# Narrow-matrix products on column tiles, with copy and transpose, and a TensorE sum for the last expert tile

## The chip, the cores and the metric

The kernel runs on one core of a Trainium2 chip. The metric is the device time of one launch in microseconds (us), lower is better. A core has five engines with queues of their own: TensorE (PE in the profile, its weight loads PEld), VectorE (DVE), ScalarE (ACT), GpSimd (POOL) and SyncE (SP), which here only issues loads and stores.

## The reference

Four batches of 512 rows of 128 values. First a cross attention with two heads of 64: keys and values are 77 context rows and the 512 rows of the batch itself. Then a mixture of eight experts of which each row takes two. Cut to its core:

```python
ln = layernorm(layernorm(x))              # latents, 512 x 128 a batch
xn = layernorm(ctx)                       # 77 x 96 a batch
q  = ln @ Wq.T
kv = concat([xn @ Wkv.T, ln @ Wlkv.T])
qn, kn = rmsnorm(q) * SCALE, rmsnorm(k)   # per head; rmsnorm needs the sum of squares of 64 values
attn = softmax(where(mask, qn @ kn.T, -big))
x = x + (attn @ v) @ Wo.T + bo
h = layernorm(x)
gates = softmax(h @ Wg + bg)              # 128 x 8
g, idx = top_k(gates, 2)
x = x + sum over the two of g * (h @ W[idx] + b[idx])
```

## The kernel before, in words

Each engine walks a list of jobs that is written out by hand in a string (TENSOR, VECTOR, SCALAR, GPSIMD). A job is a name, a part number p and a number n; a TENSOR job also names the banks of PSUM it writes (eight banks, "-" is the bank it already has). `free` (in the tensor block) makes a job wait until the former users of its banks are released, by the table RELEASED. All other order comes from semaphores that count jobs. So the lists set what is queued behind what.

The front (FRONT) has five parts: batch 0 in two halves of two tiles (p = 0, 1), then batches 1, 2 and 3 with four tiles of 128 rows each (p = 2, 3, 4). A part is normalized (`stats1` on VectorE, `rstd1` on GpSimd, `apply1` on ScalarE), transposed (`xT`, copied by `lnT`), and multiplied into `q`, `k` and `v`. Queries are squared (`qsq`), summed (`ssq`), their root taken on GpSimd (`rq`), scaled (`qn`), transposed (`qT`) and split in a high and a low half (`QH`, `QL`). Keys stay transposed: ScalarE squares them (`ksq`, inside job `k`), TensorE sums the squares of each head (`ssk`), VectorE makes means of the sums (`msk`) and GpSimd takes the root (`rk`), which is the scale of the exponentials.

In `ssk` the 128x128 tile of squared keys is the stationary matrix and `heads`, 128x2, is the moving one: four matmuls for a whole part, each of two passes in the trace, and the sums come out with rows on the partitions, as `msk` wants them (line 996). `gate` (line 1131) is built alike: four matmuls with the tile of normalized rows stationary and the 128x8 matrix `Wg0` moving; its logits go to VectorE (`logits`, `top`), with the exponential by ScalarE (`gexp`) in between, and give the weights `w`.

The rear (REAR) has one part for each batch. `score p n` (n = 0 to 4, the fifth are the context keys) takes three products for both heads; `exp` on ScalarE follows; `value p n` adds up; GpSimd and VectorE add the exponentials (`e01`, `e23`, `esum`), `den` sums them over the keys with 32 columns of ones stationary, each quarter on a column tile of its own (lines 1086 and 1091), ScalarE copies (`dens`) and `denT` transposes. `proj`, `x2`, `stats2`, `rstd2`, `apply2`, `l2T` (copied twice by ScalarE) and `l2L` lead to the experts.

The experts are computed for all rows: `low` and `high` are three matmuls of 512 columns each for four experts of one tile of rows. ScalarE scales the low four of each tile with four instructions (`low`, line 659), GpSimd adds these for a pair of tiles at once (`pair`: lines 470 and 471), VectorE scales and adds the high four with four dependent instructions for each tile (`high`, line 896), starting from `x2`, and GpSimd adds both (`res`, line 479). SyncE stores a pair of tiles after each `res`. GpSimd can't start `pair` until both tiles are scaled.

At the start, `warm` jobs are transposes of the identity that nobody reads. `ident` on GpSimd makes the identity matrix, `blanks` seven small constants; `ident` comes first. TensorE's first job waits for `ident`.

## Time and profile before

| what | value |
|---|---|
| median of 3 runs | 110.42 us (109.74 to 110.78) |
| the profiled execution | 110.81 us, its span 108.0 us |
| mean granted clock of TensorE | 0.991 |
| TensorE busy | 99.5 us (92%) |
| ScalarE busy | 83.2 us (77%) |
| GpSimd busy | 82.2 us (76%) |
| VectorE busy | 70.0 us (65%) |

The span is the time from the first to the last instruction; what lies around it is 2.8 us in this execution. The ends of matmuls are modelled, so the busy time of TensorE alone does not prove that it is the limit: its starts, and the lack of waits, have to be read with it. A time from the start of one job to the start of the next is called a step below.

### The profile page before, as it was taken

The page shows a single profiled execution, that of the slowest core. Times are in us where ns is not written, and L with a number is a line of the kernel's source. Part 1 is how long each engine was busy: PE and PEld are TensorE (multiplying, and loading weights), DVE is VectorE, ACT ScalarE, POOL GpSimd, SP SyncE. Part 2 cuts the span into 40 slices and gives each one's busy share as a digit, 9 for nine tenths or more (in the row PEclk, how much of TensorE's full clock was granted, in tenths as well). Part 3 has the DMA queues.
Part 4 walks back from the last instruction along what each step waited for, and adds up shares of the span by engine and source line. Part 5 has one row for each costly group of instructions (what it writes and reads, how often), then busy time and mean ns, then how long its engine had stood idle before and what let it go on. Part 6 is the DMA issues. An engine that isn't in the chain of part 4 may idle for free. (4 is left out here: it accounts for less than half of the span.)

```text
span 108.0 us, 2344 instructions
## 1 busy us (share of the span) xinstructions
PE 99.5 (92%) x674; PEld 69.4 (64%) x674; DVE 70.0 (65%) x327; ACT 83.2 (77%) x194; POOL 82.2 (76%) x85
## 2 busy tenths in 40 slices
...
DMA packets 6678, 3.90 MB, mean 36 GB/s; under 512 B 2314, under 2 KB 6282, under 8 KB 6667
## 3 DMA queue, kind: packets, MB, share of 16 engines
...
q10 hardware_dynamic: 832, 0.36, 1.2%
q8 instruction: 5, 0.08, 0.4%
...
HBM read 2.72 MB, written 1.05 MB: 35 GB/s over the span
## 5 line engine op out<-in xcount | busy, mean ns | idle before, releaser
L601 ACT ACTIVATE probs<-PS,shift,rk 128x512 f32<-128x512 f32 x32 | 22.5, 780 | 1.8 <-PE PS L1051 1.6
L659 ACT ACTIVATE scaled<-PS,w 128x128 f32<-128x128 f32 x64 | 17.5, 389 | 3.3 <-PE PS L920 1.9
L1072 PE MATMUL PS<-probs,V_sb 128*64 128x512 f32 x64 | 15.4, 602 | 0.0
L470 POOL TENSOR_TENSOR pair<-scaled 128x512 f32<-128x512 f32 x8 | 10.3, 1292 | 5.0 <-ACT scaled L659 4.4
L918 PE MATMUL PS<-WeH,l2H 128*128 128x512 f32 x32 | 13.3, 415 | 0.4 <-issue 0.4
L920 PE MATMUL PS<-WeH,l2L 128*128 128x512 f32 x32 | 12.6, 392 | 0.0
L919 PE MATMUL PS<-WeL,l2H 128*128 128x512 f32 x32 | 12.5, 390 | 0.0
L427 POOL TENSOR_TENSOR e<-probs,probs 128x1024 f32<-128x1024 f32 x4 | 9.5, 2368 | 3.8 <-ACT probs L601 3.8
L418 POOL TENSOR_TENSOR esum<-probs,probs 128x1024 f32<-128x1024 f32 x4 | 9.5, 2375 | 0.2 <-ACT probs L601 0.2
L457 POOL TENSOR_TENSOR l2L<-l2T,l2H 128x512 fp32r<-128x512 f32 x4 | 5.1, 1284 | 5.0 <-ACT l2H L642 5.0
L896 DVE SCALAR_TENSOR_TENSOR part<-PS,w,part 128x128 f32<-128x128 f32 x32 | 8.9, 342 | 0.0
L1072 PEld LDWEIGHTS PS<-probs,V_sb 128*64 128x64 f32 x64 | 4.1, 136 | 7.6 <-issue 7.4
L393 POOL TENSOR_TENSOR rq<-msq,half 128x8 f32<-128x8 f32 (+1 forms) x5 | 7.4, 1482 | 1.0 <-DVE msq L743 0.9
L399 POOL TENSOR_TENSOR rk<-msk,half 128x8 f32<-128x8 f32 (+1 forms) x5 | 6.9, 1389 | 1.5 <-DVE msk L759 1.5
L814 DVE TENSOR_TENSOR esum<-esum,e 128x1024 f32<-128x1024 f32 x4 | 5.0, 1249 | 4.0 <-POOL e L427 4.0
L628 ACT ACTIVATE l<-x,nm,rstd 128x127 f32<-128x127 f32 x16 | 6.6, 501 | 1.1 <-POOL nm L448 1.1
L927 PE MATMUL PS<-ident 128*128 128x128 f32 x27 | 6.0, 376 | 1.5 <-POOL ident L363 1.5
L918 PEld LDWEIGHTS PS<-WeH,l2H 128*128 128x128 f32 x32 | 6.0, 188 | 1.8 <-issue 0.6
L1051 PE MATMUL PS<-QH,KH 64*128 64x512 f32 x32 | 7.1, 443 | 0.0
L741 DVE TENSOR_REDUCE ssq<-qsq 128x8 f32<-128x512 f32 (+1 forms) x5 | 2.9, 578 | 6.2 <-ACT qsq L533 6.2
L920 PEld LDWEIGHTS PS<-WeH,l2L 128*128 128x128 f32 x32 | 6.0, 188 | 1.4
L919 PEld LDWEIGHTS PS<-WeL,l2H 128*128 128x128 f32 x32 | 6.0, 189 | 1.0
...
## 6 DMA issues: line engine op xcount, KB each, us to landing
...
```

Source lines behind the costliest of these rows:

```text
L393: pool.tensor_tensor(rq[:, b, a:e], msq[:, b, a:e], half[:, 0:H * (e - a)].rearrange("p (t h) -> p t h", h=H), ALU.pow).then_inc(rq_made, 1)
L418: pool.tensor_tensor(esum[p % 2][:, :, s], probs[p % 2][0][:, :, s], probs[p % 2][1][:, :, s], ALU.add).then_inc(e01_made, 1)
L427: pool.tensor_tensor(e23[:, :, s], probs[p % 2][2][:, :, s], probs[p % 2][3][:, :, s], ALU.add).then_inc(e23_made, 1)
L470: step(pool.tensor_tensor(pair[:], scaled[m % 2][:, :, 0:EH // 2], scaled[m % 2][:, :, EH // 2:EH], ALU.add))
L601: act.activation(probs[p % 2][n][:, h, s], ps[:, s], ACT.Exp, bias=shift[:, 0:1], scale=rk[:, b, n, h:h + 1]).then_inc(probs_made, 1)
L659: last = act.activation(scaled[m // 2 % 2][:, m % 2, e], ps[:, e], ACT.Copy, scale=w[:, m, e:e + 1])
L896: last = dve.scalar_tensor_tensor(dst, bank("high", p, 2 * n + k)[:, e * C:(e + 1) * C], w[:, m, EH + e:EH + e + 1], src, ALU.mult, ALU.add)
L918: pe.matmul(dst, lH, rH, start=True, stop=False)
L919: pe.matmul(dst, lH, rL, start=False, stop=False)
L920: return pe.matmul(dst, lL, rH, start=False, stop=True)
L1051: last = pe.matmul(bank("score", p, n, h)[0:P if n < T else M, 0:(e - a) * P], k, queries[r, b % 2, a * P:e * P], start=(step == 0), stop= ...
L1072: last = pe.matmul(bank("value", p, 0)[h * D:(h + 1) * D, s], v, pr, start=(n == 0), stop=(n == KT - 1))
```

## The change

`heads` and `Wg0` get 32 columns (the added ones are zeros). For the whole parts (p = 2, 3, 4) `ssk` takes `heads` as the stationary matrix and the 128 columns of squared keys as the moving one, four matmuls, each on its own column tile of 32, all into one bank. The result has rows of the batch along the columns, so ScalarE copies it to SBUF (`ssks`), TensorE transposes it (`sskT`), and `msk` reads the transposed one. `gate` of batches 0, 1 and 2 does the same with `Wg0` (`gates`, `gateT`). The two halves of batch 0 (`ssk`) and batch 3 (`gate`) stay as they were.

For the last tile of the last batch the high four experts are scaled by ScalarE (`high1`), and TensorE adds all eight scaled products with the identity as the stationary matrix (`sum 3 0` the low four, `sum 3 1` the high four); VectorE adds that to `x2` (`final`). The tile before it goes alone through VectorE (`high1`) and GpSimd (`pair1`, `res1`). The last pair of tiles is stored by two stores.

All four lists are written anew. Among the differences: `blanks` before `ident` on GpSimd; `warm 5` with six transposes and not four; all `score` jobs come before `low 0 1`; and batches 2 and 3 of the front are taken together.

```diff
 TENSOR = """
+    warm 4 1 7   q 0 0 4   k 0 0 5   v 0 0 6   q 1 0 7   ssk 0 0 0   k 1 0 2   v 1 0 3   warm 5 6 5   qT 0 0 5
+    xT 2 0 6   ssk 1 0 4   ctxT 0 0 0   qT 1 0 7   v 2 0 6   q 2 0 2   k 2 0 4   ctx_v 0 0 3   ctx_k 0 0 5
+    score 0 0 06   score 0 1 17   ssk 2 0 3   ctx_ss 0 0 4   maskT 0 0 5   score 0 2 06   score 0 3 34
+    sskT 2 0 5   qT 2 0 1   score 0 4 72   value 0 0 5   value 0 1 -   score 1 0 06   score 1 1 13   score 1 2 42
+    value 0 2 -   value 0 3 -   value 0 4 -   score 1 3 70   score 1 4 61   proj 0 0 32   value 1 0 4
+    value 1 1 -   den 0 0 5   value 1 2 -   denT 0 0 0   xT 3 0 7   value 1 3 -   xT 4 0 1   k 3 0 6   q 3 0 5
+    q 4 0 7   k 4 0 0   v 3 0 2   v 4 0 3   den 1 0 1   ssk 3 0 2   ssk 4 0 6   value 1 4 -   qT 3 0 0
+    sskT 3 0 2   l2T 0 0 5   denT 1 0 1   qT 4 0 3   sskT 4 0 7   score 2 0 26   score 2 1 07   gate 0 0 5
+    low 0 0 3   gateT 0 0 2   value 2 0 6   score 2 2 54   score 2 3 07   value 2 1 -   value 2 2 -
+    score 2 4 24   proj 1 0 50   score 3 0 73   value 2 3 -   value 2 4 -   score 3 1 24   score 3 2 37
+    score 3 3 01   den 2 0 5   score 3 4 62   proj 2 0 43   denT 2 0 7   low 0 1 5   low 0 2 0   low 0 3 1
+    high 0 0 2   high 0 1 6   high 0 2 3   l2T 1 0 4   high 0 3 7   value 3 0 5   value 3 1 -   value 3 2 -
+    value 3 3 -   gate 1 0 0   den 3 0 4   gateT 1 0 2   value 3 4 -   denT 3 0 6   l2T 2 0 1   proj 3 0 03
+    gate 2 0 7   high 1 0 4   gateT 2 0 5   low 1 0 2   low 1 1 1   low 1 2 7   high 1 1 0   high 1 2 3
+    high 1 3 6   high 2 0 2   low 1 3 1   low 2 0 7   l2T 3 0 0   low 2 1 4   low 2 2 1   gate 3 0 5   low 2 3 0
+    high 2 1 7   high 2 2 3   high 2 3 6   low 3 0 4   low 3 1 1   low 3 2 0   low 3 3 2   high 3 0 7
+    high 3 1 5   high 3 2 4   high 3 3 3   sum 3 0 6   sum 3 1 -
 VECTOR = """
+    consts 0 0   stats1 0 0   stats1 1 0   ln_gain 0 0   ctx_stats 0 0   stats1 2 0   ssq 0 0   gain 0 0   kL 0 0
+    ssq 1 0   shift 0 0   qn 0 0   msk 0 0   ctx_apply 0 0   qn 1 0   kL 1 0   msk 1 0   QL 0 0   stats1 3 0
+    QL 1 0   stats1 4 0   ssq 2 0   kL 2 0   ctx_kL 0 0   mask 0 0   ctx_ms 0 0   cbias 0 0   qn 2 0   msk 2 0
+    QL 2 0   esum 0 0   split 0 0   x2 0 0   stats2 0 0   esum 1 0   ssq 3 0   ssq 4 0   kL 3 0   kL 4 0   qn 3 0
+    qn 4 0   msk 3 0   QL 3 0   msk 4 0   QL 4 0   logits 0 0   top 0 0   x2 1 0   esum 2 0   stats2 1 0   x2 2 0
+    stats2 2 0   esum 3 0   high 0 0   high 0 1   logits 1 0   top 1 0   x2 3 0   stats2 3 0   logits 2 0
+    high 1 0   top 2 0   high 1 1   logits 3 0   high 2 0   top 3 0   high 2 1   high 3 0   high1 3 2   final 3 0
 SCALAR = """
+    weights 0 0   apply1 0 0   apply1 1 0   lnT 0 0   lnT 1 0   qsq 0 0   k 0 0   qsq 1 0   v 0 0   apply1 2 0
+    k 1 0   QH 0 0   lnT 2 0   v 1 0   QH 1 0   ctxT 0 0   v 2 0   weights2 0 0   qsq 2 0   k 2 0   ctx_v 0 0
+    ctx_k 0 0   exp 0 0   ssks 2 0   exp 0 1   exp 0 2   QH 2 0   exp 0 3   exp 0 4   exp 1 0   exp 1 1   exp 1 2
+    oT 0 0   exp 1 3   exp 1 4   apply1 3 0   dens 0 0   apply1 4 0   lnT 3 0   lnT 4 0   k 3 0   qsq 3 0
+    qsq 4 0   k 4 0   v 3 0   apply2 0 0   ssks 3 0   dens 1 0   v 4 0   QH 3 0   ssks 4 0   l2T 0 0   QH 4 0
+    exp 2 0   gates 0 0   oT 1 0   exp 2 1   gexp 0 0   exp 2 2   exp 2 3   low 0 0   exp 2 4   exp 3 0   oT 2 0
+    exp 3 1   exp 3 2   dens 2 0   exp 3 3   exp 3 4   apply2 1 0   low 0 1   low 0 2   l2T 1 0   low 0 3
+    apply2 2 0   gates 1 0   dens 3 0   oT 3 0   gexp 1 0   l2T 2 0   gates 2 0   low 1 0   low 1 1   low 1 2
+    apply2 3 0   gexp 2 0   low 1 3   l2T 3 0   low 2 0   low 2 1   low 2 2   low 2 3   gexp 3 0   low 3 0
+    low 3 1   low 3 2   low 3 3   high1 3 3
 GPSIMD = """
+    blanks 0 0   ident 0 0   rstd1 0 0   rstd1 1 0   ctx_rstd 0 0   rstd1 2 0   rq 0 0   rq 1 0   xbo 0 0
+    xbo 1 0   rk 0 0   rstd1 3 0   rk 1 0   rstd1 4 0   rq 2 0   ctx_rk 0 0   rk 2 0   e01 0 0   e23 0 0
+    shifted 0 0   e23 1 0   e01 1 0   xbo 2 0   rstd2 0 0   rq 3 0   rq 4 0   rk 3 0   l2L 0 0   rk 4 0   e01 2 0
+    e23 2 0   xbo 3 0   e01 3 0   rstd2 1 0   e23 3 0   rstd2 2 0   pair 0 0   res 0 0   pair 0 1   res 0 1
+    l2L 1 0   l2L 2 0   rstd2 3 0   pair 1 0   res 1 0   pair 1 1   l2L 3 0   res 1 1   pair 2 0   pair 2 1
+    res 2 0   res 2 1   pair 3 0   pair1 3 2   res 3 0   res1 3 2
...
-        Wg0 = sb("Wg0", [P, E])
+        Wg0 = sb("Wg0", [P, 32])
...
-        heads = sb("heads", [P, H])
+        heads = sb("heads", [P, 32])
...
+        ss_sb = sb("ss_sb", [P, P])
+        gate_sb = sb("gate_sb", [P, P])
...
+            if p < len(REAR) - 1:
+                held = bank("gateT", p, 0)
+                if n == 0:
+                    return held[:, 0:T * 32].rearrange("p (t k) -> p t k", k=32)[:, :, 0:E]
+                return held[:, T * 32 * n:T * 32 * n + T * E].rearrange("p (t e) -> p t e", e=E)
...
-            "ssk": lambda p, n: (msk_made, p + 1),
+            "ssk": lambda p, n: (ss_made, whole_before(p) + 1) if whole(p) else (msk_made, p + 1),
+            "sskT": lambda p, n: (msk_made, p + 1),
...
-            "gate": lambda p, n: (w_made, p + 1),
+            "gate": lambda p, n: (gates_made, p + 1) if p < len(REAR) - 1 else (w_made, p + 1),
+            "gateT": lambda p, n: (w_made, p + 1),
...
+                    last = b * T + i + 2 == B * T
                     sp.wait_ge(res_made, (b * T + i) // 2 + 1)
-                    sp.dma_start(ov[:, i:i + 2], x2[:, b, i:i + 2]).then_inc(stored, 16)
+                    tiles = slice(i, i + 1 if last else i + 2)
+                    sp.dma_start(ov[:, tiles], x2[:, b, tiles]).then_inc(stored, 16)
                     stores += 1
+            sp.wait_ge(final_made, 1)
+            sp.dma_start(ov[:, T - 1], x2[:, B - 1, T - 1]).then_inc(stored, 16)
+            stores += 1
             sp.wait_ge(stored, 16 * stores)
 
...
+                pool.memset(Wg0[:, E:32], 0.0)
...
+            def pair1_(p, n):
+
+                m = tile_number(p, n)
+                pool.wait_ge(scaled_made, m + 1)
+                pool.wait_ge(low_made, m // 2)
+                pool.wait_ge(res_made, m // 2 - 1)
+                part = scaled[m // 2 % 2][:, m % 2]
+                step(pool.tensor_tensor(pair[:, m % 2], part[:, 0:EH // 2], part[:, EH // 2:EH], ALU.add))
+                pool.tensor_tensor(low[m // 2 % 2][:, m % 2], pair[:, m % 2, 0], pair[:, m % 2, 1], ALU.add).then_inc(low_made, 1)
+
+            def res1_(p, n):
+
+                m = tile_number(p, n)
+                pool.wait_ge(low_made, m // 2 + 1)
+                pool.wait_ge(acc_made, m + 1)
+                pool.tensor_tensor(x2[:, m // T, m % T], low[m // 2 % 2][:, m % 2], acc[m // 2 % 2][:, m % 2],
+                                   ALU.add).then_inc(res_made, 1)
+
...
+            def ssks_(p, n):
+
+                act.wait_ge(ssk_done, p + 1)
+                if whole_before(p):
+                    act.wait_ge(sskT_done, whole_before(p))
+                act.copy(ss_sb[:], bank("ssk", p, 0)[:, 0:P]).then_inc(ss_made, 1)
...
+            def gates_(p, n):
+
+                act.wait_ge(gate_done, p + 1)
+                if p:
+                    act.wait_ge(gateT_done, p)
+                act.copy(gate_sb[:], bank("gate", p, 0)[:, 0:P]).then_inc(gates_made, 1)
...
+            def high1_(p, n):
+
+                m = tile_number(p, n)
+                act.wait_ge(high_done, m + 1)
+                act.wait_ge(w_made, p + 1)
+                ps = bank("high", p, n)[:].rearrange("p (e c) -> p e c", e=EH)
+                for e in range(EH):
+                    last = act.activation(scaled_high[:, e], ps[:, e], ACT.Copy, scale=w[:, m, EH + e:EH + e + 1])
+                last.then_inc(high_scaled, 1)
...
+            def high1_(p, n):
+
+                m = tile_number(p, n)
+                dve.wait_ge(w_made, p + 1)
+                dve.wait_ge(high_done, m + 1)
+                src = x2[:, m // T, m % T]
+                for e in range(EH):
+                    dst = part[m % 2][e][:] if e < EH - 1 else acc[m // 2 % 2][:, m % 2]
+                    if e == EH - 1:
+                        dve.wait_ge(res_made, m // 2 - 1)
+                    last = dve.scalar_tensor_tensor(dst, bank("high", p, n)[:, e * C:(e + 1) * C], w[:, m, EH + e:EH + e + 1], src,
+                                                    ALU.mult, ALU.add)
+                    if e < EH - 1:
+                        dve.wait_ge(dve_step, step(last))
+                    src = dst
+                last.then_inc(acc_made, 1)
+
+            def final_(p, n):
+
+                dve.wait_ge(x2_made, p + 1)
+                dve.wait_ge(sum_done, 1)
+                dve.tensor_tensor(x2[:, B - 1, T - 1], bank("sum", p, 0)[:, 0:C], x2[:, B - 1, T - 1], ALU.add).then_inc(final_made, 1)
...
+                if whole(p):
+                    for t in range(T):
+                        last = pe.matmul(bank("ssk", p, 0)[t * 32:(t + 1) * 32, 0:P], heads[:], ksq[:, b % 2, t * P:(t + 1) * P],
+                                         start=True, stop=True)
+                    last.then_inc(ssk_done, 1)
+                    return
                 for t in range(a, e):
                     last = pe.matmul(bank("ssk", p, 0)[:, (t - a) * H:(t - a + 1) * H], ksq[:, b % 2, t * P:(t + 1) * P],
-                                     heads[:], start=True, stop=True)
+                                     heads[:, 0:H], start=True, stop=True)
                 last.then_inc(ssk_done, 1)
+
+            def sskT_(p, n):
+                free("sskT", p, 0)
+                pe.wait_ge(ss_made, whole_before(p) + 1)
+                pe.transpose(bank("sskT", p, 0)[:, 0:P], ss_sb[:], ident[:]).then_inc(sskT_done, 1)
...
+                if p < len(REAR) - 1:
+                    for t in range(T):
+                        last = pe.matmul(bank("gate", p, 0)[t * 32:(t + 1) * 32, 0:P], Wg0[:], l2T[:, b % 2, t * P:(t + 1) * P],
+                                         start=True, stop=True)
+                    last.then_inc(gate_done, 1)
+                    return
                 for t in range(a, e):
                     last = pe.matmul(bank("gate", p, 0)[:, (t - a) * E:(t - a + 1) * E], l2T[:, b % 2, t * P:(t + 1) * P],
-                                     Wg0[:], start=True, stop=True)
+                                     Wg0[:, 0:E], start=True, stop=True)
                 last.then_inc(gate_done, 1)
+
+            def gateT_(p, n):
+                free("gateT", p, 0)
+                pe.wait_ge(gates_made, p + 1)
+                pe.transpose(bank("gateT", p, 0)[:, 0:P], gate_sb[:], ident[:]).then_inc(gateT_done, 1)
 
...
+            def sum_(p, n):
+
+                if n == 0:
+                    free("sum", p, 0)
+                    pe.wait_ge(scaled_made, B * T)
+                else:
+                    pe.wait_ge(high_scaled, 1)
+                parts = scaled[(B * T - 1) // 2 % 2][:, 1] if n == 0 else scaled_high
+                for e in range(EH):
+                    last = pe.matmul(bank("sum", p, 0)[:, 0:C], ident[:], parts[:, e], start=(n == 0 and e == 0),
+                                     stop=(n == 1 and e == EH - 1))
+                if n == 1:
+                    last.then_inc(sum_done, 1)
+
```

## Rows read from the trace of the kernel before

**Rows 1.** The page's first part: busy us, share of the span, instructions.
```profile
PE 99.5 (92%) x674; PEld 69.4 (64%) x674; DVE 70.0 (65%) x327; ACT 83.2 (77%) x194; POOL 82.2 (76%) x85
```

**Rows 2.** Busy time by stage, two stretches of five us (x is instructions).
```profile
70.00:75.00 5.00, 5.00 (x41) 2.85 (x41) 4.86 (x24) 1.74 (x5) 2.50 (x3) 1.00 0.00 0
...
95.00:100.00 5.00, 5.00 (x23) 4.13 (x22) 4.51 (x20) 3.29 (x14) 4.54 (x6) 1.00 0.08 26
```

**Rows 3.** Waits: who waited for what; total us, times, longest.
```profile
PEld PS L1072 <- issue: 9.7, 33, 0.4
...
PEld PS L1051 <- ACT probs L601: 1.6, 2, 0.8
```

**Rows 4.** Timeline of TensorE: start us, us, engine, line, operation, count.
```profile
36.15 0.64 PE L1086 MATMUL PS<-esum,ones 128*32 128x256 f32 x8
36.61 0.62 PE L1091 MATMUL PS<-probs,ones 77*32 77x256 f32 x8
37.15 1.05 PE L996 MATMUL PS<-heads,ksq 128*128 128x2 f32 x8
38.07 0.42 PE L1100 MATMUL PS<-ident,den_sb 128*128 128x128 f32 x2
38.32 0.60 PE L1005 MATMUL PS<-ident,qn 128*128 128x128 f32 x4
```

**Rows 5.** Timeline of TensorE around the third gate.
```profile
85.02 0.95 PE L1131 MATMUL PS<-Wg,l2T 128*128 128x8 f32 x8
85.83 0.49 PE L918 MATMUL PS<-WeH,l2H 128*128 128x512 f32 x1
```

**Rows 6.** Groups by line: busy us, mean ns; a 128x128 copy by ScalarE.
```profile
L500 ACT COPY WoT<-PS 128x128 f32<-128x128 f32 x1 | 0.3, 262 | 0.0
```

**Rows 7.** Timeline of the start, GpSimd, TensorE and ScalarE.
```profile
1.42 0.10 POOL L369 MEMSET cmv<- 77x4 f32 x1
...
1.90 0.21 POOL L372 MEMSET two<- 128x128 f32 x1
...
1.53 3.25 PE L927 MATMUL PS<-ident 128*128 128x128 f32 x14 [1.53 <-POOL ident L363]
...
4.57 0.42 PE L934 MATMUL PS<-ident,Wq_sb 128*128 128x128 f32 x1
...
5.45 0.48 ACT L495 COPY WT<-PS 128x384 f32<-128x384 f32 x1 [1.47 <-PE PS L936]
5.83 1.65 ACT L510 ACTIVATE xh<-x_sb,nm,rstd 128x128 f32<-128x128 f32 x4
```

**Rows 8.** Timeline of TensorE, the third part's queries and keys.
```profile
15.47 1.13 PE L968 MATMUL PS<-WT,lnT 128*128 128x128 f32 x8 [0.26 <-issue]
16.44 1.02 PE L977 MATMUL PS<-lnT,WT 128*128 128x512 f32 x2
```

**Rows 9.** Timeline of the tail, TensorE, ScalarE, VectorE and GpSimd.
```profile
100.68 0.39 PE L920 MATMUL PS<-WeH,l2L 128*128 128x512 f32 x1
...
101.36 0.39 PE L920 MATMUL PS<-WeH,l2L 128*128 128x512 f32 x1
...
99.07 2.17 ACT L659 ACTIVATE scaled<-PS,w 128x128 f32<-128x128 f32 x8 [0.43 <-PE PS L920]
...
103.85 0.60 DVE L896 SCALAR_TENSOR_TENSOR acc<-PS,w,part 128x128 f32<-128x128 f32 x2
...
104.44 1.40 POOL L479 TENSOR_TENSOR x<-low,acc 128x256 f32<-128x256 f32 x2
```

**Rows 10.** Timeline of the last batch's chain, VectorE, GpSimd, ScalarE.
```profile
79.07 1.13 DVE L829 SCALAR_TENSOR_TENSOR x2a<-PS,rden,xbo 128x128 f32<-128x128 f32 x4 [0.65 <-PE PS L1112]
...
82.79 0.15 DVE L848 TENSOR_REDUCE var<-mv 128x4 f32<-128x8 f32 x1
...
84.27 1.02 POOL L447 TENSOR_TENSOR rstd<-var,half 128x4 f32<-128x4 f32 x1
...
86.20 1.70 ACT L628 ACTIVATE l<-x,nm,rstd 128x127 f32<-128x127 f32 x4
```

More of the change, by code:

```diff
@@ L33 @@
-    score 1 1 14   score 1 2 07   value 0 2 -   value 0 3 -   value 0 4 -   score 1 3 14   score 1 4 07
-    den 0 0 5   ssk 3 0 6   denT 0 0 1   qT 3 0 4   proj 0 0 53   value 1 0 6   value 1 1 -   value 1 2 -
-    xT 4 0 0   score 2 0 74   score 2 1 21   score 2 2 35   k 4 0 0   q 4 0 4   den 1 0 7   score 2 3 12
-    score 2 4 07   value 1 3 -   value 1 4 -   value 2 0 3   denT 1 0 5   qT 4 0 1   ssk 4 0 2   proj 1 0 40
-    v 4 0 7   l2T 0 0 6   den 2 0 2   score 3 0 17   score 3 1 62   score 3 2 04   denT 2 0 5   low 0 0 1
@@ L38 @@
-    gate 0 0 7   score 3 3 26   value 2 1 -   value 2 2 -   value 2 3 -   value 2 4 -   value 3 0 0
-    score 3 4 42   proj 2 0 67   l2T 1 0 1   high 0 0 3   high 0 1 2   gate 1 0 4   den 3 0 1   value 3 1 -
-    value 3 2 -   value 3 3 -   value 3 4 -   denT 3 0 5   low 0 1 6   proj 3 0 71   low 0 2 2   low 0 3 3
-    low 1 0 0   l2T 2 0 4   high 0 2 6   high 0 3 2   low 1 1 1   low 1 2 5   low 1 3 7   gate 2 0 3   high 1 0 0
-    high 1 1 4   high 1 2 1   high 1 3 2   l2T 3 0 6   low 2 0 5   low 2 1 7   gate 3 0 0   low 2 2 4   low 2 3 6
@@ L660, in low_ @@
                 last.then_inc(scaled_made, 1)
-            walk(SCALAR, dict(apply2=apply2_, apply1=apply1_, weights=weights_, weights2=weights2_, lnT=lnT_, qsq=qsq_, QH=QH_, k=k_, v=v_, ctxT=ctxT_, ctx_k=ctx_k_,
-                              ctx_v=ctx_v_, exp=exp_, dens=dens_, oT=oT_, l2T=l2T_, gexp=gexp_, low=low_))
+            def high1_(p, n):
[6 more added lines that the diff above has]
+                last.then_inc(high_scaled, 1)
+            walk(SCALAR, dict(high1=high1_, apply2=apply2_, apply1=apply1_, weights=weights_, weights2=weights2_, lnT=lnT_, qsq=qsq_, QH=QH_, k=k_, ssks=ssks_, v=v_, ctxT=ctxT_, ctx_k=ctx_k_,
+                              ctx_v=ctx_v_, exp=exp_, dens=dens_, oT=oT_, l2T=l2T_, gates=gates_, gexp=gexp_, low=low_))
         @block.vector
```

77 lines of the change are left out of this document (31 added, 46 removed).

## Prediction

> **What bounds the kernel now.** Start with the page's busy shares: TensorE 92%, ScalarE 77%, GpSimd 76% [rows 1]. Since the ends of matmuls are modelled, the next view is the busy time by stage. In the middle TensorE fills all five us of a stretch while ScalarE stands idle for more than three of them, and near the end GpSimd and VectorE fill up as well (4.54 and 4.51 of 5 us) [rows 2]. The third view is the list of waits: TensorE's weight loads wait 9.7 us for "issue", in 33 pieces of at most 0.4 us, which is a load standing behind a long matmul, and the longest waits for another engine sum to 1.6 us [rows 3]. Fourth, the timeline of TensorE: one job starts where the one before lets it, with steps that repeat. The reader is to see that from about 8 us to its last expert matmul, which starts at 101.36 us and ends at 101.75 [rows 9], TensorE is the limit; everything else is arranged to be ready. After that comes a tail of VectorE, GpSimd and the store: GpSimd ends at 104.44 + 1.40 = 105.84 us, 4.1 us behind TensorE, and the span ends 2.1 us later. The chain that ended last, which the page gives by engine, reaches back only into that tail (7% of the span, GpSimd), so it would mislead if it were read alone.
>
> So the change is worth what it takes from TensorE's own sum of steps, plus what it takes from the tail, minus what comes late at the start or makes TensorE wait.
>
> **Key sums and gates on TensorE.** Before, a whole `ssk` has a step of 38.07 - 37.15 = 0.92 us [rows 4], and a gate 85.83 - 85.02 = 0.81 [rows 5] (the other two of each are within 0.13 us of these), 0.9 on average. With 2 or 8 columns moving, eight passes at 0.11 us each go mostly into loading 128 columns eight times. After, the narrow matrix is loaded and 128 columns move, on four column tiles. The nearest row is `den`: four products (eight passes) of 256 columns on column tiles take a step of 36.61 - 36.15 = 0.46 us, the second four 0.54 with the change back to the full array [rows 4]. Half the columns is at best 0.23 us; I take 0.33, with 0.1 for entering and leaving the tiled form. The transpose: two of `denT` take 38.32 - 38.07 = 0.25 [rows 4], so one is 0.13; being a job by itself it may cost a little more, 0.17. A pair costs 0.5 for 0.9 before, six pairs save 6 x 0.4 = 2.4 us. The ends: 0.23 + 0.13 = 0.36 saves 6 x 0.54 = 3.2 us; four tiles that did not overlap would take eight passes of 0.12 (a step of 16.44 - 15.47 = 0.97 for eight passes with 128 columns moving [rows 8]), 0.97 + 0.17 = 1.14, which loses 6 x 0.24 = 1.4 us. I stay near the first end, since `den` shows the overlap on this same array: eight passes with 256 columns in less time than eight with 128 on the full one.
>
> The trace shows at most 0.1 us for the switch of form. The Trainium skill, TensorEngine Tiling (Array Packing), Key Properties, says that changing the tiling mode drains TensorE, which speaks against six short tiled jobs between full ones; the `den` step agrees that there is a price, and bounds it.
>
> **The copies.** Each pair adds one 128x128 copy by ScalarE, 262 ns in the only such row [rows 6], 6 x 0.26 = 1.6 us on an engine with 108.0 - 83.2 = 24.8 idle us [rows 1], and two more handoffs (TensorE to ScalarE to TensorE) of about 0.1 us, so the sums and logits come some 0.5 us later after their job. The new lists put other TensorE work between the two halves of a pair: scores between `ssk 2` and `sskT 2`, a `low` between `gate 0` and `gateT 0`, `den 3` between `gate 1` and `gateT 1`. That work hides it. Without cover a pair would stop TensorE for about 0.5 us, 3 us in all, and eat the gain. `gates` and `ssks` wait at the head of ScalarE's queue; behind `ssks 2` stands `exp 0 1`, behind `gates 0` `oT 1`, both with scores already queued.
>
> **The start.** `blanks` moves ahead of `ident`. In the trace the blanks stand behind the identity, begin at 1.42 and end at 1.90 + 0.21 = 2.11 us [rows 7]. So the identity comes 0.7 us later, and the new memset of `Wg0` adds up to 0.1. TensorE's first 14 transposes take from 1.53 to 4.57, then follow the weights' transposes, then ScalarE's copy of them at 5.45, and right behind it in its queue `apply1` at 5.83 [rows 7], whose input was ready before. Nothing there has slack, so the first queries start about 0.65 us later. I take 0.6; the bounds are 0 (if the weights' load lands so late that the transposes waited for it anyway) and 0.75. `warm 5` has two transposes more, 2 x 0.12 by the passes of [rows 8], 0.2 us.
>
> **The new order between.** I walked the TensorE list by steps and asked at each job what it waits for. The front is shorter ahead of the first score, because `ssk 2` and `ctx_ss` stand behind it, so exponentials begin about a us earlier. I found no long wait: a few tenths at `v 2`, at `score 1 2` (banks), and the largest at `gate 3`, where ScalarE still copies `l2T 3` behind `apply2 3`, `gexp 2` and `low 1 3`, about 0.3 us. I take 0.4 us for all, bounds 0 and 2.5 (this part is the least certain; it is worked out for five queues at once).
>
> **The tail.** Before, from the end of TensorE at 101.75 to the last `res` at 105.84 it is 4.09 us [rows 9]. After, the last tile goes: four ScalarE instructions, 2.17 / 2 = 1.09 us [rows 9]; handoff 0.1; four products with the identity, eight passes, 0.97 [rows 8], and 0.1 to their end; VectorE's add like half of the two that took 0.60 [rows 9], 0.3, and handoffs 0.15. Sum 2.7 us, a gain of 1.4. But ScalarE is close to late here: behind `l2T 3` it has low 2 (4 x 1.09), low 3 (4 x 1.09) and high1 (1.09), 9.8 us, and a wait of some tenths for the last weights, against fourteen expert jobs and a gate on TensorE, 14 x 0.68 [rows 9] + 0.8 = 10.3 us. I put 0.2 us on the tail for that. GpSimd loses half of its last pair's work, and begins the pairs about eight us earlier against the end, since `low 0 1` comes long before `value 3`; it is no limit any more. `final` waits at the end of VectorE's queue with nothing behind it. The store of the last tile has half the bytes; I leave its 2.1 us unchanged, since the time from issue to landing of a store this size is latency for the most part.
>
> **Sum.** -2.4 (pairs) +0.2 (warm) +0.6 (start) +0.4 (waits) -1.4 (tail) +0.2 (ScalarE late) = -2.4 us on the span of 108.0: 105.6, and 110.8 - 2.4 = 108.4 for an execution like the profiled one. That one lies 0.4 above the median, so the forecast is 110.4 - 2.4 = 108.0 us.
>
> **Rivals.** (a) The pairs cost only their lower end and the start is hidden: another -0.8 and -0.6, and no waits, -0.4: 106.2 us. For it: TensorE's steps repeat within 0.1 us wherever the form is the same. Against: the start's chain in [rows 7] has no gap.
> (b) Slower: batch 3's chain takes over. Between `proj 3` and `l2T 3` stand `x2`, `stats2`, `rstd2` and `apply2`. In the trace VectorE's part runs from 79.07 to 82.79 + 0.15 = 82.94, 3.9 us; GpSimd's root and product 1.3; ScalarE's four 1.7 [rows 10]; with `proj` and handoffs 8.3 us. In the new list TensorE has `proj`, a gate pair and ten experts there, 1.1 + 0.5 + 10 x 0.68 [rows 9] + 0.2 for changes of form = 8.6 us. So it decides from 0.3 us of queueing on: before `rstd2 3` GpSimd must do `l2L 2`, before `apply2 3` ScalarE does three `low`. In the trace GpSimd came 1.3 us late to this root and ScalarE 0.6 late to the job behind it [rows 10], because others stood in front. If the pair's delays (0.5 each for `gates 1` and `gates 2`) and one GpSimd pair job (2 us) come on top, TensorE stops for 3 us there and the tail's ScalarE comes 1 us later: 108.0 + 4 = 112.0 us.
> (c) ScalarE becomes the bound in the middle. All scores of batches 2 and 3 stand before `low 0 1`, so ten exponential jobs with two copies, a `low` and a gate copy run there against TensorE's scores and values, both some 16 us long, with banks that let TensorE lead by two scores. If its copies, exponentials and the `low` outrun TensorE by a tenth of that stretch, 1.6 us are lost: 109.6 us; twice that, 111.2. The Trainium skill, TensorEngine Tiling (Array Packing), PSUM Bottleneck, says that after such a speedup the copy out of PSUM may become the bottleneck, which is this rival; the idle time of ScalarE in [rows 1] speaks against it on the whole, not in this stretch.
> (d) The column tiles don't overlap for 128 columns: the 2.4 us gain turns into a loss of 1.4, 108.0 + 3.8 = 111.8 us. `den` speaks against it.
>
> **How the numbers follow.** Within 1% of 110.4 is about what a measurement of this kernel can tell from no change, 109.3 to 111.5 us. Chances: my forecast, 107.0 to 109.3 with its small terms, 0.54; (a) 0.20; (c) 0.14; (b) 0.08; (d) 0.04. The range for 8 in 10 runs from 106.0, between (a) and its far end, to 110.6, over (c). Faster: 0.54 + 0.20 = 0.74; the same: 0.15, which is (c) with a little of (b); slower: 0.11.
>
> **What would show it.** `ssk` of the whole parts with a step near 0.33 us and transposes near 0.17; TensorE's first key or query matmul near 8.9 us and not 8.3; the last expert matmul ending near 100.3; the span's end some 4.9 us after it. TensorE's waits by other engines should stay under 2 us in sum. The prediction is wrong if TensorE waits for `l2T 3` or `gate 3` by more than a us, if steps of the tiled jobs are near 0.9, or if ScalarE's last job ends more than 1.5 us behind TensorE's last expert matmul.

## The result, and the profile after

The changed kernel takes 113.25 us (median of 4 runs, 112.93 to 113.40) against 110.08 us (4 runs, 109.73 to 110.78) for the kernel before: a ratio of 1.028, 95% interval 1.023 to 1.034. It is slower by 2.8%. The forecast was 108.0 us, range 106.0 to 110.6, so both sign and range are wrong.

The span of the profiled execution is 111.1 us, 108.0 before. The page's first part and its row of TensorE's granted clock, which answer to [rows 1]:

```profile
PE 100.8 (91%) x698; PEld 67.8 (61%) x698; DVE 76.4 (69%) x324; ACT 85.5 (77%) x204; POOL 83.7 (75%) x86
...
PEclk9999985999999999999999999999999999999999
```

VectorE is busy 6.4 us more with three instructions fewer, and no edit gives it 6 us of work: that is the first thing to see. The second is the clock, below 9 tenths in two slices of the forty, the sixth and seventh, between 13.9 and 19.4 us, and nowhere else. TensorE's count of instructions and busy time say little.

Next, the timeline of TensorE in the changed kernel, from `ctxT` to the first scores, around the tiled jobs, in the middle, and at the end (start us, us, engine, line, operation, count, and in brackets the idle time before it with what ended it):

```profile
15.72 0.72 PE L1122 MATMUL PS<-ident,cxh 77*96 77x77 f32 x4 [1.88 <-DVE cxh L874]
...
16.66 1.91 PE L1085 MATMUL PS<-WT,lnT 128*128 128x128 f32 x8
18.36 1.38 PE L1067 MATMUL PS<-WT,lnT 128*128 128x128 f32 x8
19.58 1.02 PE L1076 MATMUL PS<-lnT,WT 128*128 128x512 f32 x2
...
21.93 0.50 PE L1161 MATMUL PS<-QH,KH 64*128 64x512 f32 x2
...
23.51 0.43 PE L1096 MATMUL PS<-ksq,heads 128*32 128x128 f32 x8
23.87 0.71 PE L1145 MATMUL PS<-heads,cksq 128*77 128x2 f32 x8
...
26.26 0.33 PE L1108 MATMUL PS<-ident,ss_sb 128*128 128x128 f32 x1
26.42 0.60 PE L1115 MATMUL PS<-ident,qn 128*128 128x128 f32 x4
...
51.02 0.43 PE L1096 MATMUL PS<-ksq,heads 128*32 128x128 f32 x8 [0.78 <-DVE KL L842]
...
104.34 0.40 PE L1019 MATMUL PS<-WeH,l2L 128*128 128x512 f32 x1
105.10 1.13 PE L1275 MATMUL PS<-scaled,ident 128*128 128x128 f32 x8 [0.36 <-DVE acc L972]
```

The tiled jobs do what was forecast: `ssk 2` has a step of 23.87 - 23.51 = 0.36 us and `sskT 2` one of 26.42 - 26.26 = 0.16, together 0.52 where 0.92 stood before [rows 4]. The loss has its start at 15.72 us. TensorE stands 1.88 us for `ctxT`, whose input is `cxh` (the normalized context of `ctx_apply`), and `v 2`, two jobs behind it, eight passes, has a step of 18.36 - 16.66 = 1.70 us where the same form took 0.97 [rows 8]. The first score starts at 21.93 us; in the kernel before it started at 19.66:

```profile
19.66 0.50 PE L1051 MATMUL PS<-QH,KH 64*128 64x512 f32 x2
```

VectorE and GpSimd of the changed kernel around that time and in the middle, from the same timeline:

```profile
12.55 3.02 DVE L874 TENSOR_SCALAR cxh<-ctx_sb,cmv,crstd 77x96 f32<-77x96 f32 x4
13.02 2.49 POOL L466 TENSOR_TENSOR xbo<-x_sb,bo_b 128x512 f32<-128x512 f32 x2 [0.46 <-DMA bo_b<-in_L_xattn_bo_dram]
...
33.15 2.37 POOL L405 TENSOR_TENSOR We<-We_sb,We_end 128x1024 f32<-128x1024 f32 x1
33.28 3.32 DVE L888 TENSOR_TENSOR esum<-esum,e 128x1024 f32<-128x1024 f32 x1 [4.62 <-POOL e L454]
35.48 1.19 POOL L406 TENSOR_TENSOR Wg<-Wg_sb,Wg_end 128x8 f32<-128x8 f32 x1
...
39.61 2.81 POOL L445 TENSOR_TENSOR esum<-probs,probs 128x1024 f32<-128x1024 f32 x1
40.23 3.27 DVE L789 TENSOR_TENSOR WeL<-We,WeH 128x1024 fp32r<-128x1024 f32 x1
43.42 0.24 DVE L899 RECIPROCAL rden<-PS 128x4 f32<-128x4 f32 x2
```

And the same groups of instructions by line in the kernel before (busy us, mean ns), rows that the prediction didn't read:

```profile
L814 DVE TENSOR_TENSOR esum<-esum,e 128x1024 f32<-128x1024 f32 x4 | 5.0, 1249 | 4.0 <-POOL e L427 4.0
L720 DVE TENSOR_TENSOR WeL<-We,WeH 128x1024 fp32r<-128x1024 f32 x1 | 1.2, 1224 | 0.0
L718 DVE CAST WeH<-We 128x1024 fp32r<-128x1024 f32 x1 | 1.1, 1111 | 0.0
L800 DVE TENSOR_SCALAR cxh<-ctx_sb,cmv,crstd 77x96 f32<-77x96 f32 x4 | 1.0, 321 | 0.0
```

The same instructions on the same shapes: `cxh` takes 3.02 us for 1.0, `esum 0` 3.32 for 1.25, `WeL` 3.27 for 1.22, and `WeH` 1.86 for 1.11 (that 1.11 was lengthened too: in the last kernel below `WeH` takes 0.76). Each long one lies beside a large GpSimd instruction that reads SBUF, and its length is near "the rest of GpSimd's instruction, then its own time": `esum 0` begins 0.13 us into the 2.37 us of `We`, the large add of the job `shifted`, so 2.24 + 1.22 = 3.46 for 3.32. What lies beside GpSimd without harm is as telling: four statistics of rows take 0.87 us from 46.09, beside `xbo` from 46.23, and 0.87 from 88.32, where GpSimd stands idle, and `x2`, with an input in PSUM, takes 1.13 us for four instructions from 43.77, where GpSimd stands idle, and 1.13 from 85.99, beside `l2L`. GpSimd pays as well when it comes second: the tiny `Wg` of `shifted` took 1.19 us here and 0.20 in an experiment below where VectorE did something else, and `e01 1` took 2.81 where its like takes 2.37.

The trace of before already held the sign. Timeline of GpSimd and VectorE there:

```profile
44.69 2.00 POOL L447 TENSOR_TENSOR rstd<-var,half 128x4 f32<-128x4 f32 x1
...
44.48 1.32 DVE L814 TENSOR_TENSOR esum<-esum,e 128x1024 f32<-128x1024 f32 x1
```

Four elements per partition, and 2.00 us beside an `esum`, where [rows 10] has 1.02 for the same instruction. So VectorE and GpSimd shut each other out for certain pairs of instructions, and the new lists put such pairs side by side. The Trainium skill, SBUF — State Buffer, section "Who interferes with whom", states it as an exclusive lock on a pair of ports that both engines use: whoever issues first holds it for the whole instruction, and it is asked for by a VectorE instruction with two inputs in SBUF (against a GpSimd instruction that reads SBUF), and by a copy, cast or `tensor_scalar` in a two-port mode, but not by one with at most one input in SBUF outside those modes. The four lengthened forms are two with two SBUF inputs, a cast and a `tensor_scalar`, and the rows above agree. One does not fit "for the whole instruction": in the fourth kernel below `cxh` runs from 9.09 to 10.13 us beside a `rstd` of four elements from 9.25, and they take 1.04 and 1.02 us, both their usual times. So a small GpSimd instruction did not hold VectorE up. That the lock is the mechanism, and not another way of shutting out, no run here shows.

### The profile page after: what moved, and what is told of

Read it like the earlier page. It is cut to its first block and busy times, and to the rows that moved or that the text cites. A ratio compares the mean times of both kernels' runs of the same rounds, so it can differ in the third digit from the quotient of the medians.

```text
span 111.1 us, 2413 instructions
## 1 busy us (share of the span) xinstructions
PE 100.8 (91%) x698; PEld 67.8 (61%) x698; DVE 76.4 (69%) x324; ACT 85.5 (77%) x204; POOL 83.7 (75%) x86
## 5 line engine op out<-in xcount | busy, mean ns | idle before, releaser
L1182 PE MATMUL PS<-probs,V_sb 128*64 128x512 f32 x64 | 15.9, 608 | 0.0
L466 POOL TENSOR_TENSOR xbo<-x_sb,bo_b 128x512 f32<-128x512 f32 x4 | 5.9, 1481 | 6.0 <-DVE x L907 5.5
L888 DVE TENSOR_TENSOR esum<-esum,e 128x1024 f32<-128x1024 f32 x4 | 7.0, 1742 | 4.6 <-POOL e L454 4.6
L497 POOL TENSOR_TENSOR pair<-scaled 128x512 f32<-128x512 f32 x7 | 9.0, 1288 | 0.1
L474 POOL TENSOR_TENSOR rstd<-var,half 128x4 f32<-128x4 f32 x4 | 5.9, 1475 | 4.2 <-DVE var L922 4.2
L903 DVE SCALAR_TENSOR_TENSOR x2a<-PS,rden,xbo 128x128 f32<-128x128 f32 x16 | 4.5, 345 | 5.0 <-PE PS L1222 4.7
L972 DVE SCALAR_TENSOR_TENSOR part<-PS,w,part 128x128 f32<-128x128 f32 x28 | 7.8, 341 | 0.0
L413 POOL TENSOR_TENSOR rstd<-var,half 128x4 f32<-128x4 f32 (+1 forms) x5 | 4.4, 888 | 4.4 <-DVE var L804 4.4
L420 POOL TENSOR_TENSOR rq<-msq,half 128x8 f32<-128x8 f32 (+1 forms) x5 | 6.9, 1386 | 0.3 <-DVE msq L812 0.3
```

Source lines behind the costliest of these rows:

```text
L497: step(pool.tensor_tensor(pair[:], scaled[m % 2][:, :, 0:EH // 2], scaled[m % 2][:, :, EH // 2:EH], ALU.add))
L888: dve.tensor_tensor(esum[p % 2][:, :, s], esum[p % 2][:, :, s], e23[:, :, s], ALU.add).then_inc(esum_made, 1)
L972: last = dve.scalar_tensor_tensor(dst, bank("high", p, 2 * n + k)[:, e * C:(e + 1) * C], w[:, m, EH + e:EH + e + 1], src, ALU.mult, ALU.add)
L1182: last = pe.matmul(bank("value", p, 0)[h * D:(h + 1) * D, s], v, pr, start=(n == 0), stop=(n == KT - 1))
```

## The experiments

Ten kernels ran. Ratios are to the kernel before on the same chip, with the 95% interval. None is 2% away from 1; whether one differs from 1 is read from its interval.

| kernel | us (before) | ratio |
|---|---|---|
| lists of before, pairs alone | 109.14 (109.74) | 0.994 [0.991, 0.997] |
| lists of before, tail alone | 110.00 (109.74) | 0.998 [0.993, 1.003] |
| changed, `xbo` later | 110.62 (109.74) | 1.006 [1.004, 1.008] |
| changed, `ctx_apply` earlier | 109.96 (109.74) | 1.000 [0.998, 1.002] |
| and `split` earlier | 108.62 (109.72) | 0.990 [0.987, 0.993] |
| `ctx_apply` earlier, old tail | 110.58 (109.72) | 1.008 [1.005, 1.011] |
| both earlier, final store first | 108.55 (109.72) | 0.989 [0.986, 0.991] |
| both earlier, old `ssk` and `gate` | 110.98 (109.72) | 1.011 [1.008, 1.014] |
| both earlier, stores, `ident` first | 108.39 (109.72) | 0.986 [0.981, 0.990] |
| lists of before, pairs and tail | 108.42 (109.72) | 0.987 [0.983, 0.991] |

**Parts alone in the lists of before.** The first kernel inserts the six pairs at the places of the old jobs, the second takes only the new tail:

```diff
 TENSOR (pairs)
-    ssk 2, ssk 3, ssk 4, gate 0, gate 1, gate 2 as one job each
+    sskT 2 behind score 0 1, sskT 3 behind qT 3, sskT 4 behind proj 1
+    gateT 0 behind score 3 3, gateT 1 behind den 3, gateT 2 behind high 1 0
 TENSOR, VECTOR, GPSIMD (tail)
+    sum 3 0 4   sum 3 1 -
-    high 3 1            pair 3 1   res 3 1
+    high1 3 2 final 3 0   pair1 3 2   res1 3 2
```

> The lists of the kernel before, with only the six pairs put in (ssk and gate on column tiles, copy by ScalarE, transpose into the same bank a few jobs later); start order, warm and tail as before. Theory A (the pairs do what they cost in the sum; the loss comes from the new lists): each pair's two steps on TensorE sum to 0.5 us or a little less, TensorE's last expert matmul ends 2 to 2.5 us before 101.75, and as the tail is bound by GpSimd and VectorE only 1 to 2 us of it reach the end: 108.3 to 109.5 us, ratio 0.98 to 0.995. Rival B (the pairs' longer chain through ScalarE makes TensorE wait): 110.5 to 112 us, with waits for ss_sb or gate_sb.

Measured 0.994. The time is in theory A's range, but its step on TensorE is not: the last expert matmul ends at 100.59 + 0.40 = 100.99 us, 0.76 before that of the old kernel, where 2 to 2.5 were expected. Half of the 0.76 was there before any pair: the first key matmul starts at 7.90 us, for 8.29. TensorE's waits in this kernel, by place (total us, times, longest):

```profile
PE PS L1013 <- ACT scaled L714: 0.5, 1, 0.5
PE PS L1206 <- ACT den_sb L660: 0.4, 1, 0.4
```

With a third, of 0.3 us for issue, these are 1.2 us, where the kernel before waits 0.6 us in the same stretch, for issue alone. That the other engines' work was timed to the old steps fits these two, but they are half a us; where the rest of the expected 2 us went stays open.

> The lists of the kernel before, with only the last tile's sum on TensorE (high1, sum, final, pair1, res1, three last stores in place of two). Theory A (the tail is held by GpSimd's list and by SyncE's stores in line, as the changed kernel's trace shows: res1 ends 1.0 us after final there and the store of final is issued 0.5 us after that): the end moves by less than 1 us, 109.6 to 110.6 us, ratio 0.993 to 1.004. Rival (the forecast's 1.4 us): 109.0 us, 0.987.

Measured 0.998: no difference, which is theory A's number. Its mechanism is borne out in half. In the profiled execution the last `res1` ended at 104.01 + 0.46 = 104.47 us, 0.2 us behind `final` and 1.4 us before the old `res` [rows 9], so GpSimd did not hold the tail here, yet the span is 107.9. SyncE's queue there:

```profile
104.93 1.34 SPq L370 DMA_DIRECT2D out_dram<-x  x1
```

The last store is issued last and took 1.34 us to issue, where the other kernels with this tail show 0.45. Nine of the ten executions, without the slowest, spread from 108.86 to 110.45 us, so the gain may be there in some of them and not in others. What makes that store slow stays open.

**The start: `cxh` beside `xbo`.** Two ways to part them, each with the changed kernel otherwise:

```diff
 GPSIMD (third kernel)
-    rstd1 2   rq 0   rq 1   xbo 0   xbo 1   rk 0 ...  e01 0   e23 0   shifted 0   e23 1   e01 1
+    rstd1 2   rq 0   rq 1   rk 0 ...  e01 0   xbo 0   e23 0   shifted 0   e23 1   e01 1   xbo 1
 VECTOR (fourth kernel)
-    stats1 2   ssq 0   gain 0   kL 0   ssq 1   shift 0   qn 0   msk 0   ctx_apply 0   qn 1
+    stats1 2   ctx_apply 0   ssq 0   gain 0   kL 0   ssq 1   shift 0   qn 0   msk 0   qn 1
```

> The changed kernel, with GpSimd's xbo 0 and xbo 1 moved behind e01 0 and e01 1, so that no large GpSimd add runs beside VectorE's ctx_apply; VectorE's list untouched. Theory A (VectorE and GpSimd exclude each other for operations that read SBUF twice or copy fast, so ctx_apply's four instructions stood 2 us behind xbo): the four take about 1.05 us in all and not 3.0, TensorE waits less than 0.5 us for ctxT, v 2 takes a step of 0.9 and not 1.7 since the granted clock does not fall: first score near 19.5 and not 21.9 us; 110.5 to 111.8 us, ratio 1.003 to 1.015. Rival (ctx_apply is just placed too late in VectorE's list): its instructions stay near 3 us or ctxT still waits over 1.5 us, time unchanged at 113.2.

> The changed kernel, with VectorE's ctx_apply moved up to behind stats1 2 (where the kernel before has it), ahead of GpSimd's xbo. Theory A: its four instructions take 1.05 us, no wait of ctxT, no fall of the granted clock, the first score near 19.3 us, and 110.0 to 111.5 us (ratio 1.00 to 1.013): the rest of the loss stays, since it is further on. Rival (the front's delay is given back anyway because a later stage is bound elsewhere): 112.5 to 113.3 us.

`cxh` took 1.04 us in both. The third kernel leaves VectorE's list alone, so it was GpSimd's neighbour and not the place in VectorE's list that made `cxh` late. With `ctx_apply` earlier the time is 109.96 us, 3.3 less than the changed kernel (3.1 by the ratios 1.028 and 1.000), and the span 107.8, 3.3 less. Timeline of TensorE and VectorE in that kernel:

```profile
9.09 1.04 DVE L873 TENSOR_SCALAR cxh<-ctx_sb,cmv,crstd 77x96 f32<-77x96 f32 x4
...
13.79 0.45 PE L1121 MATMUL PS<-ident,cxh 77*96 77x77 f32 x4
...
14.51 1.13 PE L1084 MATMUL PS<-WT,lnT 128*128 128x128 f32 x8
15.47 1.06 PE L1066 MATMUL PS<-WT,lnT 128*128 128x128 f32 x8
16.36 1.02 PE L1075 MATMUL PS<-lnT,WT 128*128 128x512 f32 x2
...
18.71 0.50 PE L1160 MATMUL PS<-QH,KH 64*128 64x512 f32 x2
```

The first score is 3.22 us earlier: `ctxT` starts 1.93 earlier (13.79 for 15.72), it and `qT 1` take 0.72 for 0.94, `v 2` 0.96 for 1.70, `q 2` 0.89 for 1.22. The last three, 1.3 us, are steps of the same instructions at different speed. Busy time by stage, from 15 to 20 us, of the changed kernel and then of this one (span, busy us of TensorE, its loads, VectorE, ScalarE, GpSimd; granted clock; DMA share and GB/s):

```profile
15.00:20.00 5.00, 4.28 (x23) 4.09 (x24) 4.85 (x26) 2.20 (x6) 3.18 (x5) 0.66 0.62 71
```

```profile
15.00:20.00 5.00, 5.00 (x38) 3.81 (x36) 4.42 (x23) 4.43 (x12) 4.87 (x6) 1.00 0.41 86
```

The 0.66 is a mixture of the two levels (1.2 and 2.4 GHz). The same view of the changed kernel, cut more finely:

```profile
13.80:15.70 1.90, 0.04 (x1) 0.01 (x1) 1.90 (x3) 0.78 (x2) 1.90 (x3) 0.98 0.99 214
15.70:19.00 3.30, 3.28 (x17) 3.30 (x18) 3.23 (x18) 1.35 (x3) 1.56 (x2) 0.50 0.75 75
```

The clock was at the higher level until just before the end of a stretch in which TensorE stood, and at the lower one for the 3.3 us behind it; in the fourth kernel it is 1.00 throughout. So a wait of under two us cost over three.

Both kernels did better than expected at the first score (19.5 and 19.3 us) and the fourth came in 0.04 us under its range. Moving `xbo` gave 110.62, 0.7 us more than moving `ctx_apply`, although the first score is as early (18.56): `xbo 1` then ran at 39.72 in the middle, beside `WeL`, took 2.25 us and added a wait of 0.65 us for `x` of the first batch. The collision was moved, not removed.

**The middle: `esum`, `WeH`, `WeL` beside the shifts.** On top of the fourth kernel:

```diff
 VECTOR
-    QL 2   esum 0   split 0   x2 0
+    QL 2   split 0   esum 0   x2 0
 GPSIMD
-    rk 2   e01 0   e23 0   shifted 0   e23 1   e01 1
+    rk 2   shifted 0   e01 0   e23 0   e23 1   e01 1
```

> As e4, and in addition GpSimd's shifted moved from behind e23 0 to behind rk 2, and VectorE's split from behind esum 0 to ahead of it, so that VectorE's three large SBUF operations (esum 0, and the two of split) stand less behind GpSimd's. Theory A (VectorE came 2 us late to x2 0 because these three took 8.3 us and not 3.6, and that is the wait of TensorE at ssk 4 and qn 4 and the late start of score 2 0): x2 0 starts about 38.2 and not 40.2 us, score 2 0 1 to 2 us before 51.6, 108.0 to 109.2 us, ratio 0.983 to 0.994. Rival (TensorE's waits there come from ScalarE or from the key sums' detour): within 0.3 us of e4, 109.9.

Measured 108.62 us, 1.3 less by the medians and 1.1 by the ratios, 0.9899 for 0.9999. VectorE's timeline in this kernel:

```profile
30.95 3.29 DVE L788 TENSOR_TENSOR WeL<-We,WeH 128x1024 fp32r<-128x1024 f32 x1
34.16 1.21 DVE L887 TENSOR_TENSOR esum<-esum,e 128x1024 f32<-128x1024 f32 x1
38.58 0.25 DVE L898 RECIPROCAL rden<-PS 128x4 f32<-128x4 f32 x2 [3.21 <-PE PS L1209]
```

`esum 0` is back at 1.21 us. `WeL` is still long, beside `e23 0`, but where VectorE has time: it then waits 3.21 us for TensorE, where in the changed kernel it went without a gap from `WeL` to `rden` at 43.42. `x2 0` thus comes 1.6 us earlier than in the fourth kernel, and TensorE's wait of 0.78 us for `KL` of batch 3 is gone; one of 0.45 us for `msk` is left. What counts is whether a lengthened instruction has slack, not whether there is one.

**The pairs, priced in these lists.** The fifth kernel with `ssk` and `gate` as they were, each in the place and the bank of its transpose, without the copies:

```diff
 TENSOR
-    ssk 2 ... sskT 2 0 5   ssk 3 0 2 ... sskT 3 0 2   gate 0 0 5 ... gateT 0 0 2   (and so on)
+    ssk 2 0 5              ssk 3 0 2                  gate 0 0 2
```

> As e5, with the six pairs undone: ssk 2, 3, 4 and gate 0, 1, 2 in the old form (large tile stationary), standing where the transposes stood and in their banks, without ScalarE's copies. TensorE has 2.4 us more work by the rows. Theory A (from score 2 0 on TensorE is the limit, so its own work counts in full): 1.2 to 2.4 us above e5, about 110.5. Rival (the copies and handoffs cost as much as they save): within 0.5 us of e5.

Measured 110.98 us, side by side with the fifth: the pairs are worth 110.98 - 108.62 = 2.36 us, against the forecast's 6 x 0.4 = 2.4. That is a net price. The fifth kernel has a wait of 0.45 us for `msk`, at the end of the longer chain over ScalarE, and the one without pairs has none there, only one of 0.16 us elsewhere, for exponentials. By these numbers the steps alone gave some 0.3 us more than was forecast, and the longer chain took it back.

**The tail, priced in these lists.** The fourth kernel with the old tail:

```diff
 TENSOR
-    sum 3 0 6   sum 3 1 -
 VECTOR, SCALAR, GPSIMD
-    high1 3 2   final 3 0   /   high1 3 3   /   pair1 3 2   res1 3 2
+    high 3 1                /               /   pair 3 1   res 3 1
```

> As e4, with the last tile as before (high 3 1, pair 3 1, res 3 1, one store; no sum on TensorE). The forecast's term says that the sum is worth 1.4 us less 0.2: 111.1 us. Theory A (GpSimd and SyncE hold the tail in both forms): within 0.6 us of e4, 109.5 to 110.6 us, ratio 0.998 to 1.006.

Measured 110.58 for 109.96: the tail is worth 0.6 us (0.8 by the ratios, 1.0075 for 0.9999). The next kernel asked whether the rest is lost in SyncE's queue, where the last tile's store stands third:

```diff
+                    if last:
+                        sp.wait_ge(final_made, 1)
+                        sp.dma_start(ov[:, T - 1], x2[:, B - 1, T - 1]).then_inc(stored, 16)
                     sp.wait_ge(res_made, (b * T + i) // 2 + 1)
...
-            sp.wait_ge(final_made, 1)
-            sp.dma_start(ov[:, T - 1], x2[:, B - 1, T - 1]).then_inc(stored, 16)
```

> As e5, with SyncE waiting for final and storing that tile ahead of the last two stores of GpSimd's tiles. In e4 final ended at 104.28 us, but its store was issued last, at 105.72, behind two others of 0.45 us each. Expected if the queue of issues holds the end: 0.4 us less than e5, ratio 0.003 to 0.005 lower. If the store of res1 (issued at about 105.3 then) decides by its landing alone: no difference.

Measured 108.55, 0.07 less, where 0.4 was expected: a miss. Its end, from the timelines of VectorE, GpSimd and SyncE's queue:

```profile
102.81 0.29 DVE L1000 TENSOR_TENSOR x<-PS,x 128x128 f32<-128x128 f32 x1 [0.60 <-PE PS L1275]
...
103.65 0.45 POOL L523 TENSOR_TENSOR x<-low,acc 128x128 f32<-128x128 f32 x1
...
103.72 0.33 SPq L372 DMA_DIRECT2D out_dram<-x  x1
104.10 0.43 SPq L368 DMA_DIRECT2D out_dram<-x  x1
104.57 0.46 SPq L372 DMA_DIRECT2D out_dram<-x  x1
```

The last tile is ready at 103.10, its neighbour, GpSimd's, at 104.10. Only the order of two stores was changed: the last tile's now goes at 104.10, but `res1` of the neighbour ends then, and its store leaves 0.47 us later, as the last one did in the fifth kernel (104.72, with `res1` at 104.25).

**The start, and the old lists.** The seventh kernel with `ident` ahead of `blanks` (the diff), and the lists of before with both pairs and tail (the two edits of the first diff together):

```diff
 GPSIMD
-    blanks 0 0   ident 0 0
+    ident 0 0   blanks 0 0
```

> As e7, with ident ahead of blanks again on GpSimd. The forecast priced blanks first at 0.6 us of the start. Against it: in the changed kernel's trace the first q starts at 8.37 us, in e1 and e2, with ident first, the first k at 7.90 and 7.98, and in the kernel before at 8.29. Expected: first q near 7.9 to 8.3, so 0 to 0.4 us less than e7 (108.5), ratio 0.985 to 0.989. If the start's delay is real and carried through: 0.6 us less.

> The lists of the kernel before with both the six pairs and the last tile's sum put in: the change without its new lists. e1 alone gave 0.6 us, e2 alone 0.2 us within its uncertainty. If both add: 108.9 us, ratio 0.990 to 0.995. If the shorter TensorE now lets the tail's sum pay (it starts earlier while GpSimd has half a pair less): 108.3 to 108.7.

Measured 108.39 and 108.42 us. With `ident` first the first queries start at 7.98 us and not at 8.61 (the seventh kernel), 0.63 earlier, but the first score starts at 18.92 and not at 18.86, and the time differs by 0.16 us by the medians and 0.34 by the ratios (0.9856 for 0.9887), inside the uncertainty, since these intervals reach 0.3 to 0.5 us to each side. TensorE's waits in that kernel tell why:

```profile
PE PS L1115 <- DVE qn L820: 0.7, 1, 0.7
```

`qn` starts on VectorE at 12.45 us in this kernel and at 12.39 in the seventh, no earlier. VectorE goes there without a gap from the statistics of the context, which waited for their input and began at 6.58 and 6.39; that they set its time is argued, not shown. The 0.63 us end as a wait. The old lists with both edits are 1.3% faster than before (0.983 to 0.991), more than the 0.6% and 0.2% of the parts, though within their intervals; the second of the two expected figures, 108.3 to 108.7, fits. The new lists with the same edits are 2.8% slower: the whole loss is in the lists, and the mended new lists (108.39 to 108.62) are no better than the old ones.

## Why the prediction was wrong

The forecast was a change of -2.4 us and +3.2 was measured (113.25 - 110.08), so 5.6 us are to be found. The start's collision is 3.1 to 3.3 of them, the middle's 1.1 to 1.3 (by ratios and by medians), the tail's missing gain 0.4 to 0.6. That makes 4.6 to 5.2; the rest, 0.4 to 1.0 us, stays open. It is luck that 108.0 + 3.3 + 1.3 + 0.6 is 113.2: the forecast counted from 110.4, and the kernel before took 109.7 to 110.1 in the comparisons here.

**The step that failed** is "The new order between": "I take 0.4 us for all, bounds 0 and 2.5". The walk through the queues took every VectorE and GpSimd job with its duration in the trace of before, as if that didn't depend on what runs beside it. It found "a few tenths at `v 2`" and not the 1.88 us two jobs ahead of it. Nor did the walk price what a wait does to the clock: 1.3 of the 3.2 us at the start. TensorE's waits by other engines sum to 3.2 us from 8 us on (1.88, 0.78, 0.36, 0.18), over the 2 us that were named as the sign. With both collisions out of the way the term comes near what it measures, 0.65 us for 0.4: the fifth kernel has waits of 0.45 and 0.20 us from 8 us on.

**The pairs**: right. Forecast 0.5 a pair and 2.4 us in all; the steps are 0.36 and 0.16, and undoing them costs 2.36. That the total fits to 0.04 us is in part luck, as the price above shows. Rival (d) is excluded, since tiles that did not overlap would have a step of 0.97.

**The copies**: nearly right. Under the jobs between the halves they are hidden, but for the wait of 0.45 us for `msk` in the mended lists; the price above contains it.

**The start**: forecast 0.6, and first queries "near 8.9 us and not 8.3". In the changed kernel they start at 8.37 us, for 8.29 before. The delay itself came: TensorE's first transposes start at 2.20 us for 1.53 and those of the weights at 5.24 for 4.57, 0.67 later. But the next two transposes, of `Wlkv_sb`, have a step of 5.64 - 5.42 = 0.22 us where they had 5.21 - 4.78 = 0.43 before, and so on to the first queries, although the page's row has the clock at full speed there in both. When these steps get short varies among the kernels here: with `blanks` first the first job starts at 8.30 to 8.65 us, with `ident` first at 7.90 to 8.29. The two that differ in nothing else are 0.63 us apart (8.61 and 7.98), near the term, but "nothing there has slack" ended at the first query: five us on, `qn` is no earlier, and of the term the 0.16 to 0.34 us are left that the uncertainty covers.

**The tail**: mis-sized. Forecast a gain of 1.4, less 0.2 for ScalarE. TensorE and VectorE did their part nearly as worked out, 107.60 - 104.74 = 2.86 us from the last expert matmul to the end of `final`, for 2.7 + 0.2. What failed is "it is no limit any more" of GpSimd. Timeline of the changed kernel's tail, ScalarE, VectorE, GpSimd and SyncE's queue, which answers to [rows 9]:

```profile
104.78 1.21 ACT L728 ACTIVATE scaled_high<-PS,w 128x128 f32<-128x128 f32 x4
...
107.31 0.29 DVE L1000 TENSOR_TENSOR x<-PS,x 128x128 f32<-128x128 f32 x1 [0.59 <-PE PS L1275]
...
104.00 1.29 POOL L497 TENSOR_TENSOR pair<-scaled 128x512 f32<-128x512 f32 x1
...
106.23 0.73 POOL L515 TENSOR_TENSOR pair<-scaled 128x256 f32<-128x256 f32 x1
...
107.45 0.72 POOL L506 TENSOR_TENSOR x<-low,acc 128x256 f32<-128x256 f32 x1
108.13 0.45 POOL L523 TENSOR_TENSOR x<-low,acc 128x128 f32<-128x128 f32 x1
...
109.05 0.45 SPq L372 DMA_DIRECT2D out_dram<-x  x1
```

GpSimd goes through these jobs without a gap and ends at 108.58, a us behind `final`; one more store is issued behind it at 109.05. The lead of "about eight us" that the forecast gave it was 3 at the outset and was then waited away. The first `pair` starts at 79.04 us, 25.7 ahead of TensorE's last expert matmul, where it was 79.19 and 22.6 before. GpSimd's timeline further on:

```profile
89.94 1.02 POOL L474 TENSOR_TENSOR rstd<-var,half 128x4 f32<-128x4 f32 x1 [2.70 <-DVE var L922]
```

So it stands 2.70 us for batch 3's `rstd2` with `pair 1 0` queued behind it, and from there to its end it has no gap over 0.26 us: it is a limit again. From TensorE's last expert matmul to the end of the span it is 6.4 us (6.2 before), not the forecast's 4.9.

**The other rivals.** (b) and (c) didn't happen: no wait for `l2T 3` or `gate 3` is in the trace, and from 70 to 75 us TensorE is as full as in [rows 2]. For (c) little room was left, though: ScalarE is busy for all five us there, for 1.74 before. Of (a) only the hidden start came. The slower case had a chance of 0.11, made of mechanisms on other engines; none was on the pair that collided.
